# A Householder step reordered: column sums read before the second update, u and y formed from root and sign, and w's row by a transpose

## The reference, cut to what matters

```python
L_norm = d_inv_sqrt[:, None] * L * d_inv_sqrt[None, :]
_, U = jnp.linalg.eigh(L_norm)
agg = jnp.einsum('mn,bnd->bmd', U.T, features)
h = jax.nn.relu(agg @ W1 + b1)
out = h @ W2 + b2
return jnp.einsum('nm,bmd->bnd', U, out)
```

## Time and profile before

| what | value |
|---|---|
| median of 3 runs | 965.54 us |
| lowest, highest | 964.47, 966.66 us |
| span of the profiled execution | 962.9 us, 13676 instructions |
| the profiled execution's own time | the profile gives its span alone; the median of the runs is 2.6 us above it |
| TensorE busy (matmul) | 810.6 us, 84% |
| VectorE busy | 758.1 us, 79% |
| ScalarE busy | 502.6 us, 52% |
| GpSimd busy | 168.7 us, 18% |
| mean granted TensorE clock | 0.961 of full speed |

### The profile page before, as it was taken

How to read it: one execution, slowest core, us unless ns; L and a number is a source line. 1 busy time by engine, 2 the same in 40 slices (tenths; PEclk the granted TensorE clock), 3 DMA queues, 4 the chain that set the end, 5 groups by cost and what they waited for, 6 DMA issues and landing times. The chain is left out here.

```text
span 962.9 us, 13676 instructions
## 1 busy us (share of the span) xinstructions
PE 810.6 (84%) x3862; PEld 535.5 (56%) x3862; DVE 758.1 (79%) x3165; ACT 502.6 (52%) x1106; POOL 168.7 (18%) x397
## 2 busy tenths in 40 slices
PE   4579998888999999999999997758882868889898
PEld 3468774434444466666555453736661655566565
DVE  6877777887888778888888888968989989869633
ACT  0037875554444434444433433148881776788675
POOL 2111111111111211211212120002202333071000
PEclk9999999999999979999999999879996988999999
DMA  9000000000000000000000000000000000000022
GB/s 281 14 1 1 2 1 1 1 1 0 1 1 0 1 1 1 0 1 1 2 0 1 1 1 0 1 0 1 1 1 1 1 0 1 1 1 1 22 77 77
DMA packets 13970, 12.16 MB, mean 13 GB/s; under 512 B 1092, under 2 KB 10823, under 8 KB 13895
## 3 DMA queue, kind: packets, MB, share of 16 engines
q1 hardware_dynamic: 10704, 8.46, 3.0%
q10 hardware_dynamic: 3190, 2.84, 1.0%
HBM read 7.10 MB, written 4.19 MB: 12 GB/s over the span
## 5 line engine op out<-in xcount | busy, mean ns | idle before, releaser
L565 ACT ACTIVATE G<-bank,bias 128x512 f32<-128x512 f32 (+1 forms) x252 | 158.6, 636 | 234.7 <-PE bank L662 197.1
L662 PE MATMUL bank<-HT,wih 128*128 128x512 f32 (+1 forms) x504 | 250.5, 583 | 0.5 <-ACT HT L551 0.5
L432 POOL TENSOR_TENSOR col_root<-sa,neg_half 128x1 f32<-128x1 f32 x126 | 79.5, 631 | 484.4 <-DVE sa L907 484.4
L662 PEld LDWEIGHTS bank<-VI 128*128 128x128 f32 x506 | 94.5, 202 | 120.2 <-DVE VI L905 57.8
L662 PE MATMUL bank<-H,whh 128*128 128x512 f32 (+1 forms) x288 | 136.2, 555 | 2.6 <-DVE H L905 2.6
L662 PE MATMUL bank<-VI 128*128 128x129 f32 (+63 forms) x506 | 95.4, 272 | 22.3 <-DVE VI L905 22.2
L521 ACT ACTIVATE T<-X,nbias,rstd 128x128 f32<-128x128 f32 x256 | 104.7, 487 | 5.1 <-DVE nbias L906 5.1
L525 ACT COPY T<-bank 128x512 f32<-128x512 f32 x128 | 75.0, 586 | 56.2 <-PE bank L662 41.8
L662 PEld LDWEIGHTS bank<-XI,A 128*128 128x128 f32 x252 | 41.1, 201 | 89.3 <-DVE A L906 87.5
L662 PEld LDWEIGHTS bank<-HT,wih 128*128 128x128 f32 x504 | 80.8, 195 | 10.3 <-issue 4.4
L672 PE MATMUL bank<-ident,T 128*128 128x128 f32 x256 | 40.7, 288 | 52.1 <-ACT T L608 43.4
(11 more groups left out here) (339 smaller groups left out, 1559.4 us busy)
## 6 DMA issues: line engine op xcount, KB each, us to landing
out_x<-T SPq DMA_DIRECT2D x16, 256.0 KB, 2.3
wih<-in_WihT ACTq DMA_DIRECT2D x1, 1024.0 KB
whh<-in_WhhT ACTq DMA_DIRECT2D x1, 1024.0 KB
qkvT<-in_WqkvT ACTq DMA_DIRECT2D x1, 192.0 KB
wg<-in_Wg ACTq DMA_DIRECT2D x2, 64.0 KB
l3w<-in_L3W ACTq DMA_DIRECT2D x2, 64.0 KB
adjT<-in_adjT ACTq DMA_DIRECT2D x1, 64.0 KB
adj<-in_adj SPq DMA_DIRECT2D x1, 64.0 KB, 2.1
```

Of the source, the lines that this page charges most:

```text
L432: e.tensor_tensor(out=col["root"][:, :], in0=sa[:, 0:1], in1=neg_half[:, :], op=ALU.pow).then_inc(root_ready, 1)
L565: e.activation(G[x.h][:, gate, 0:n], gate_bank(k)[:, 0:n], ACT.Tanh if gate == 2 else ACT.Sigmoid, bias=bias[:, 4 * (x.p - 1) + gate:4 * ( ...
L662: mm = lambda out, l, r, start=True, stop=True: e.matmul(out, l, r, start=start, stop=stop)
```

## The change

The three sums of step i + 1 are read into `sa` before the second update of step i, not behind it; GpSimd's root waits for nothing else. Three VectorE instructions behind the update take from `sa` the sign (as +1 or -1), the size, and a flag with the factor -1. The copy of gx and the forming of c go: u and y are XI and gx (straight from bank 1) times root times sign, v and p are two instructions instead of one, a1 is size times root plus 1. GAM gets a second plane for the flag, and its product is formed once behind the last step. w's row is made by a transpose of w, 128 columns in one pass. The LSTM's forget product moves from before the second update to a new place 3 behind it. The diff, cut to its core:

```diff
-                    e.wait_ge(p_ready, i)
+                    e.wait_ge(p_ready, 2 * i)
                     e.tensor_copy(out=XI[(i + 1) % 2][:, 2:3], in_=ident[:, ds(i + 2, 1)]).then_inc(oh_ready, 1)
...
-                    mm(bank[7][:, i + 1:P], bc(VI[:, 1, i + 3:i + 4]), VI[:, 0, i + 3:P + 2]).then_inc(wr_ready, 1)
+                    e.transpose(bank[7][:, 0:P], bc(VI[:, 1, i + 3:i + 4]), ident[:, :]).then_inc(wr_ready, 1)
...
-                if place == 2:
+                if place in (2, 3):
                     for x in PRODUCT_AT.get(i, []):
...
-                        if x.s:
+                        elif x.s:
                             e.wait_ge(l_act, x.k0 + 3)
                             TT(T[h][4][:, 0:n], G[h][:, 1, 0:n], C[h][:, 0:n], ALU.mult).then_inc(l_fc, 1)
...
-                    link(TT(A1[:, :], GAM[:, :], ident[:, :], ALU.mult))
+                    link(STT(A1[:, :], GAM[:, 0, :], -1.0, GAM[:, 1, :], ALU.mult, ALU.mult))
+                    link(TT(A1[:, :], A1[:, :], ident[:, :], ALU.mult))
...
+            def column_sums(i):
+
+                e.wait_ge(s_ready, i + 1)
+                TS(sa[:, :], bank[0][:, 0:3], 1e-30, None, ALU.add).then_inc(sa_ready, 1)
+
+            def column_signs(i):
+
+                e.wait_ge(sa_ready, i + 1)
+                link.note(e.tensor_scalar(c("signed").bitcast(U32), sa[:, 2:3].bitcast(U32), 0x80000000, 0x3f800000, ALU.bitwise_and, ALU.bitwise_or))
+                link.note(e.tensor_scalar(c("size").bitcast(U32), sa[:, 2:3].bitcast(U32), 0x7fffffff, None, ALU.bitwise_and))
+                return link.note(TS(GAM[:, 1, i:i + 1], sa[:, 1:2], 1e-30, -1.0, ALU.is_gt, ALU.mult))
...
-                    e.wait_ge(s_ready, i + 1)
-                    TS(sa[:, :], bank[0][:, 0:3], 1e-30, None, ALU.add).then_inc(sa_ready, 1)
                 first_mixer(i, 0)
                 if hh:
...
+                    e.wait_ge(ch_e, signs_done)
+                    e.wait_ge(root_ready, i + 1)
+                    made_u = link.note(TS(u, xi[:, 0:1], c("root"), c("signed"), ALU.mult, ALU.mult))
                     e.wait_ge(gx_ready, i + 1)
-                    link.note(e.tensor_copy(out=xi[:, 3:5], in_=bank[1][:, 0:2]))
-                    e.wait_ge(root_ready, i + 1)
-                    link(e.tensor_scalar(c("c").bitcast(U32), sa[:, 2:3].bitcast(U32), 0x80000000, c("root").bitcast(U32), ALU.bitwise_and, ALU.bitwise_or))
-                    link(TS(u_y, xi[:, 0:4:3], c("c"), None, ALU.mult))
-                    TT(v_p, u_y, xi[:, 2:5:2], ALU.add).then_inc(p_ready, 1)
-
-                    link(TS(c("a1"), sa[:, 2:3], c("c"), 1.0, ALU.mult, ALU.add))
-                    link(e.reciprocal(out=c("rec"), in_=c("a1")))
-                    k = link.note(STT(gam, sa[:, 1:2], 1e-30, c("rec"), ALU.is_gt, ALU.mult))
-                    e.wait_ge(ch_e, k)
-                    e.wait_ge(p_ready, i + 1)
-                    TS(w3, v, gam, -1.0, ALU.mult, ALU.mult).then_inc(w_ready, 1)
+                    made_y = link.note(TS(y, bank[1][:, 0:1], c("root"), c("signed"), ALU.mult, ALU.mult))
+                    made_a1 = link.note(TS(c("a1"), c("size"), c("root"), 1.0, ALU.mult, ALU.add))
+                    e.wait_ge(ch_e, made_u)
+                    TT(v, u, xi[:, 2:3], ALU.add).then_inc(p_ready, 1)
+                    e.wait_ge(ch_e, made_y)
+                    TT(p, y, bank[1][:, 1:2], ALU.add).then_inc(p_ready, 1)
+                    e.wait_ge(ch_e, made_a1)
+                    made_gam = link.note(e.reciprocal(out=gam, in_=c("a1")))
+                    e.wait_ge(ch_e, made_gam)
+                    e.wait_ge(p_ready, 2 * i + 2)
+                    TS(w3, v, gam, live, ALU.mult, ALU.mult).then_inc(w_ready, 1)
...
+                if i + 1 < STEPS:
+                    column_sums(i + 1)
                 if hh:
                     e.wait_ge(ch_e, a)
                     e.wait_ge(wr_ready, i + 1)
                     STT(A[:, rest], bank[7][:, rest], c("q"), A1[:, rest], ALU.mult, ALU.add).then_inc(a_ready, 1)
+                if i + 1 < STEPS:
+                    signs_done = column_signs(i + 1)
+                if hh:
                     e.wait_ge(a_ready, i + 2)
+                first_mixer(i, 3)
```

More of the change, by code:

```diff
@@ L297, in build @@
         adj, A, A1, Ln = [sb(n, [P, P]) for n in "adj A A1 Ln".split()]
-        XI = [sb(f"XI{i}", [P, 5]) for i in range(2)]
-        VI, GAM = sb("VI", [P, 2, P + 2]), sb("GAM", [P, P])
+        XI = [sb(f"XI{i}", [P, 3]) for i in range(2)]
+        VI, GAM = sb("VI", [P, 2, P + 2]), sb("GAM", [P, 2, P])
         V = VI[:, 0, 1:P + 1]
@@ L302, in build @@
         col = {n: sb("col_" + n, [P, 1]) for n in (
-            "deg rowsum diag pos inv dinv root c a1 rec q sgm mxe mxd mnd lo w cnt1 frac d_at d_up lam mn idx ss inr lmax sign gcol").split()}
+            "deg rowsum diag pos inv dinv root signed size a1 q sgm mxe mxd mnd lo w cnt1 frac d_at d_up lam mn idx ss inr lmax sign gcol").split()}
         Nm, NT, XT, VT, D_, QT, TT_ = [sb(n, [P, P]) for n in "Nm NT XT VT D_ QT TT_".split()]
@@ L408, in _ @@
             e.memset(neg_half[:, :], -0.5).then_inc(s_pool, 1)
-            e.memset(GAM[:, STEPS:P], 0.0).then_inc(s_pool, 1)
+            e.memset(GAM[:, :, STEPS:P], 0.0).then_inc(s_pool, 1)
             e.iota(iota_f[:, :], pattern=[[1, P]], base=0, channel_multiplier=0, allow_small_or_imprecise_dtypes=True).then_inc(s_pool, 1)
@@ L960, in first_mixer @@
                 j = i - STATS_AT
-                if 0 <= j < 8:
+                if 0 <= j < 8 and place < 3:
                     e.wait_ge(x_in[j // 2], 16)
@@ L979, in first_mixer @@
                     TT(half4(T[g % 2][4]), half4(bank[5]), bias1[:, :].unsqueeze(1).to_broadcast([P, GB, P]), ALU.add).then_inc(a_b1, 1)
-                if place == 2:
+                if place in (2, 3):
                     for x in PRODUCT_AT.get(i, []):
                         u, h, n = x.index, x.h, x.n
[L983 to L986, removed]
-                        if x.s:
+                        if place == 2:
+                            e.wait_ge(l_act, x.k0 + 2)
+                            if u >= 2:
+                                e.wait_ge(l_h, u - 1)
+                            TT((T[h][2] if x.s else C[h])[:, 0:n], G[h][:, 0, 0:n], G[h][:, 2, 0:n], ALU.mult).then_inc(l_ig, 1)
+                        elif x.s:
                             e.wait_ge(l_act, x.k0 + 3)
@@ L1114, in tridiagonal @@
                     link(e.tensor_copy(out=n2[:, :, 1], in_=ne2p[:, P // 2 + 1:P + 1][:, ::-1]))
+            def column_sums(i):
[6 more added lines that the diff above has]
+                return link.note(TS(GAM[:, 1, i:i + 1], sa[:, 1:2], 1e-30, -1.0, ALU.is_gt, ALU.mult))
             TT(XI[0][:, 0:2], A[:, 0:1].to_broadcast([P, 2]), low[:, 0:2], ALU.mult).then_inc(x_ready, 1)
+            column_sums(0)
+            signs_done = column_signs(0)
             for i in range(FIRST_MIXER_STEPS):
@@ L1137, in _ @@
-                    link(TS(c("a1"), sa[:, 2:3], c("c"), 1.0, ALU.mult, ALU.add))
-                    link(e.reciprocal(out=c("rec"), in_=c("a1")))
-                    k = link.note(STT(gam, sa[:, 1:2], 1e-30, c("rec"), ALU.is_gt, ALU.mult))
-                    e.wait_ge(ch_e, k)
-                    e.wait_ge(p_ready, i + 1)
-                    TS(w3, v, gam, -1.0, ALU.mult, ALU.mult).then_inc(w_ready, 1)
+                    xi, gam, live, rest = XI[i % 2], GAM[:, 0, i:i + 1], GAM[:, 1, i:i + 1], slice(i + 1, P)
@@ new lines, in _ @@
+                    u, v = VI[:, 0, i + 2:i + 3], VI[:, 0, i + 1:i + 2]
+                    p, y, y_w, w3 = VI[:, 1, i + 1:i + 2], VI[:, 1, i + 2:i + 3], VI[:, 1, i + 2:i + 4], VI[:, 1, i + 3:i + 4]
+                    e.wait_ge(ch_e, signs_done)
+                    e.wait_ge(root_ready, i + 1)
+                    made_u = link.note(TS(u, xi[:, 0:1], c("root"), c("signed"), ALU.mult, ALU.mult))
+                    e.wait_ge(gx_ready, i + 1)
+                    made_y = link.note(TS(y, bank[1][:, 0:1], c("root"), c("signed"), ALU.mult, ALU.mult))
```

## The result

The changed kernel takes 926.77 us (median; 925.69 to 931.49) against 965.53 (964.47 to 966.66): ratio 0.9611, 95% interval 0.9593 to 0.9629. That is 38.8 us less, where 46.3 were forecast: inside the range, 8 us short of the point. The profiled span fell from 962.9 to 925.9, 37.0 us.

The account below looks back on a forecast made before the run. Bound by VectorE's single chain per Householder step, with TensorE second and full at four pieces a step. Terms 3.6 + 1.6 + 13.9 + 7.1 + 16.6 + 3.8 - 0.3 = 46.3, so 965.5 - 46.3 = 919 us; range 908 to 939.

Parts of the forecast that it names:

- steps 0 to 11: Statistics steps: two links go, root already hidden, k then bounds XI; 0.3 x 12 = 3.6 us.
- graph: Steps 12 to 27, graph layers: TensorE and ScalarE bound, only w's transpose counts; 0.1 x 16 = 1.6 us.
- length 1: Steps 28 to 44, LSTM window length 1: shorter VectorE chain, step 4.60 to 3.76; 0.82 x 17 = 13.9 us.
- length 2: Steps 45 to 67, LSTM window length 2: four of six steps TensorE-full, mean 4.25; 0.31 x 23 = 7.1 us.
- length 3: Steps 68 to 99, LSTM window length 3: shorter pieces, mean step 3.85; 0.52 x 32 = 16.6 us.
- length 4: LSTM window length 4: nearly all steps have four pieces, 4.42 becomes 4.27; 0.15 x 25 = 3.8 us.
- rest: At the end: one added 128x128 instruction for GAM, costing 0.3 us.
- rival one: VectorE instructions do not overlap, leaving only the moved sa and hidden signs: some 25 us, 940; chance 0.10.
- Rival two: GpSimd's root and VectorE's two-input products block each other, costing 5 to 10 us: 924 to 929; chance 0.10.
- Rival three: TensorE loses its clock under the new order; 110 us more at the low level gives 975; chance 0.03.
- Rival four: Steps are TensorE-bound in more places, lengths 2 to 4 stay but for 0.1: 938; chance 0.07.
- the 4.25 that I had named as a sign of error: Steps with four LSTM pieces on TensorE: expected at 4.3 us, forecast wrong if they come out below 4.25.

Follow-up runs that it names:

- e5: Changed kernel with the two waits in front of u swapped, the root's first, then the signs'; 926.25 us, ratio 0.9605 to the kernel before.
- e12: Changed kernel with the flag added into size by one instruction between the signs' and root's waits, w with one pointer scalar; 923.24 us, ratio 0.9563.
- e3: Changed kernel with GpSimd's copy of the unit column set ahead of the root instead of behind it; 927.33 us, ratio 0.9597.
- e8: Changed kernel with one pointer scalar instead of two in u, y and w, output not the reference's; 918.29 us, ratio 0.9512.
- e6: Changed kernel with the LSTM's forget product back ahead of the sums and second update; 933.70 us, ratio 0.9663.
- e7: Changed kernel with the old chain back (copy of gx, c, joint u and y, joint v and p, flag in gam); 947.91 us, ratio 0.9806.
- e1: Changed kernel with w's row made by the old two-pass product instead of the transpose; 937.26 us, ratio 0.9690.
- e4: Changed kernel with the sums read behind the second update instead of ahead of it; 932.70 us, ratio 0.9661.
- e10: Changed kernel with two more instructions beside the root, u and w with one pointer scalar, signs' wait ahead of the mixer's work; 940.42 us, ratio 0.9743.

## Why the prediction was right, and where 8 us went

The terms of the forecast beside the profiled executions; they add up to 46.3 and 37.0 us, and 1.8 more lie between the span's gain and the medians'.

| term | forecast | measured | |
|---|---|---|---|
| steps 0 to 11 | 3.6 | -0.4 | full matmul speed came 4 us later; 1.5 where it didn't (e5), still under half |
| graph | 1.6 | 2.0 | right |
| length 1 | 13.9 | 7.9 | the mis-sized term |
| length 2 | 7.1 | 7.3 | mean step 4.25, by errors that cancel |
| length 3 | 16.6 | 17.5 | right in size, 2.6 of it from the clock |
| length 4 | 3.8 | 5.2 | step 4.21, forecast 4.27 |
| rest | -0.3 | -2.4 | clock 0.91 against 0.92; 377.0 to 381.5 us in the kernels here |

**The chain of length 1** is the step that was off, in two sizes. "u starts at +0.82, where col_c did" took col_c's 0.03 behind the root for u, which has several waits in one row in front of it: 0.10 (e12 against the changed kernel; the order alone is 0.04 in e5, and GpSimd's copy and the second pointer are excluded by e3 and e8). The two-pointer instruction was put at 0.13, between the bounds of 0.07 and 0.23: it is 0.19, and 0.06 in w as well (e8). Together 0.10 + 2 x 0.06 + 0.06 = 0.28 against 0.26 missing at XI. Fifteen steps by 0.21 (0.61 won instead of 0.82) are 3 us. The other 3 us are steps 28 and 29, where 1.6 were due and 1.2 were lost: the granted clock is 0.73 there in the kernel after. These are its windows, the two steps and the rest after the last root:

```profile
148.45:160.90 12.45, 11.78 (x30) 5.88 (x30) 6.48 (x36) 7.57 (x10) 1.37 (x4) 0.73 0.00 0
...
546.40:925.90 379.50, 295.50 (x1654) 217.53 (x1652) 294.80 (x1075) 244.51 (x659) 67.73 (x122) 0.91 0.04 12
```

In the kernel before the same two steps take 11.2 us at 0.85. The kernels here fall into two groups, 10.9 to 11.2 us and 12.2 to 12.5, and the groups go by when step 28 starts: 148.5 us or earlier gives the long time (8 kernels), 149.3 or later the short one (6). Why that is so stays open, and the 3 us are the luck of where this stretch begins, not a price of the new links.

**Length 2 came out by luck.** The forecast's own terms give (3 x 4.29 + 4.7 + 2 x 3.8) / 6 = 4.20, not the 4.25 it took. Measured are 3.97 to 4.00 in the steps with three pieces (3.8 forecast), 4.85 to 4.87 in the longest of the six (4.7; once 4.67) and 4.14 to 4.27, once 4.44, in the other four-piece steps (4.29): two terms too low, one too high. **Steps 0 to 11**: the early steps gained 0.15 each where 0.3 was put, and no run says why; the rest of the miss is the full speed that came later. The forecast also read TensorE's part in the waits too small: 10.7 us in 16 steps is A's update alone, and with gx and XI it was 46.5.

**Instructions overlap**, as rival one denied: v and p start 0.06 apart though each takes 0.15. The Trainium skill's page "VectorE: DVE Perf Modes" says in "The DRAIN you can't avoid" that a semaphore after each of eight copies cost nothing extra. No run here prices a semaphore's signal by itself. Waits in a row in front of an instruction are another thing, and they cost: 0.10 in the changed kernel against e12.

**Rival two is out.** The forget product started inside a root; VectorE's timeline of the kernel after, then GpSimd's:

```profile
533.97 0.68 DVE L905 TENSOR_TENSOR T<-G,C 128x512 f32<-128x512 f32 x1
```

```profile
533.81 0.55 POOL L432 TENSOR_TENSOR col_root<-sa,neg_half 128x1 f32<-128x1 f32 x1 [3.53 <-DVE sa L907]
534.31 0.39 POOL L436 COPY XI<-ident 128x1 f32<-128x1 f32 x1
```

It began 0.16 into the root. Neither was stretched; the copy behind the root was, from 0.18 to 0.39, and nobody waits for it. In e6 the cell sum, the instruction that stretched 34 roots in the kernel before, starts 0.15 to 0.23 into the root in 34 steps, and every root still takes 0.55. The Trainium skill's page "SBUF — State Buffer", section "Who interferes with whom", has a two-input VectorE instruction and a GpSimd one that reads SBUF block each other: the copy's row agrees, the root's row doesn't, in this order of starts, while the earlier trace rows do in the other.

**Rival three is out**: the mean granted clock is 0.959 against 0.961, and at the start of length 3 the clock doesn't fall in this kernel, which is luck (e3, e6). In the kernel before, step 70 takes 6.41 us and its like eight steps on (78) 3.86; after, 3.66 and 3.64. The 2.6 us are part of length 3's gain: without them it is 14.9, against 16.6 forecast. **Rival four is out**: lengths 2 and 3 gave 24.8 us. The four-piece step lies below the 4.25 that I had named as a sign of error: the transpose also shortens the issue of the s matmul behind it by 0.08.

**What each part is worth**, from undoing it: the shorter chain 21 us (e7), the transpose 10 (e1; about 7 without TensorE's late full speed), the forget product behind the update 7 (e6), the sums ahead 6 (e4). They add to 44, more than the 38.8 in all. Undoing one also changes the luck of the clock that goes with the kernel: e1 has 63.0 and 80.5 in the first two columns, and e3, whose edit gives nothing, has 1.4 less in length 1 and 1.4 more in length 3.

## What to carry to other kernels

When you take a start from the row of another instruction, compare the waits in front of both: several in one row cost 0.10 us here, and an instruction that had to be done anyway, put between them, gave it back. A wait that others fill is only room up to its end: two small instructions moved beside the root ended 0.14 behind it and made the kernel 9 us slower, 14 with a wait moved up as well. Where two engines take turns at being last, price each stretch by itself. In the chain the forecast missed at the two places for which it had no row, the start of u and the two-pointer instruction. And cut two kernels at the same steps before you compare them: the clock alone moved single stretches by 1 to 3 us here, in kernels whose edits had nothing to do with it.

## What the runs showed of the hardware that was not expected

- A VectorE instruction with two pointer scalars lasts 0.27 us and holds the next for 0.19; with one, 0.21 and 0.12 to 0.13 (e8).
- Three waits in one row in front of an instruction start it 0.13 to 0.14 behind GpSimd's root, in 66 of 66 steps; the root's wait second to last, 0.09 to 0.10; one wait, 0.03 to 0.04 (changed kernel, e5, e12).
- A root that starts while a wide VectorE sum with both inputs in SBUF is running takes 0.75 or 0.94 instead of 0.55 (34 of 34 in the kernel before). Beside a wide sum that reads one of its two inputs from a bank, where TensorE writes, it takes 0.55 (16 of 16). The same cell sum starting 0.15 to 0.23 into the root stretches neither (e6), nor does the forget product in the changed kernel.
- A one-pass transpose issues in 0.11, and the short two-pass matmul behind it in 0.14 instead of 0.22 (e1 against the changed kernel).
- Eight 128-column matmuls take 2.06 us before and 1.14 after a point that lies between 63 and 77 us in the kernels, with a granted clock of 1.00 in the records on both sides. In e10 the short time comes at 70.7, is gone at 72.9 and is back at 76.9. TensorE's timeline of the kernel after; in e5 the same change of speed comes 5 us earlier, with 1.9 us less in steps 8 to 11:

```profile
66.66 2.06 PE L662 MATMUL bank<-adjT,T 128*128 128x128 f32 x8
...
71.10 1.14 PE L662 MATMUL bank<-adjT,T 128*128 128x128 f32 x8
```
